# Scores of a cross-attention block: one float32 product per part, or three float32r products of split operands

## The chip, the cores and the metric

The kernel runs on one core of one Trainium2 chip. The metric is the device time of one execution in microseconds (us). Three executions of the kernel before took 1213.2, 1216.02 and 1218.1 us; the median is 1216.02 us.

The engines go by short names: PE is TensorE (PEld its weight loads), DVE is VectorE, ACT is ScalarE, POOL is GpSimd, SP is SyncE, which here does nothing but wait and issue DMAs.

## The reference

`x` has shape (2, 2048, 512), the context (2, 77, 512). One layer is computed:

```python
xn = layernorm(x)
q = (xn @ Wq.T + bq)   # 16 heads of 32
k = (ctx @ Wk.T + bk)
v = (ctx @ Wv.T + bv)
scores = q @ k.T / sqrt(32) + causal      # causal: column s > row t is -inf
x = x + softmax(scores) @ v @ Wo.T + bo
h = silu(q4(layernorm(x)) @ q4(w_gate).T) * (q4(layernorm(x)) @ q4(w_up).T)
out = x + q4(h) @ q4(w_down).T            # q4: blockwise FP4 quantise and dequantise, blocks of 16
```

FF width is 1408. Only the first 77 rows of a batch are touched by the causal mask.

## The kernel before, in words

The 4096 rows are 32 tiles of 128 rows (`T = 32`, 16 per batch). The program has two parts: attention over all 32 tiles (to about 437 us), then the feed-forward part over the same tiles. The change touches the first alone.

Every engine runs its own program, written out by hand; `iteration(a, n)` of an engine is what it does in turn `a`. In one turn several tiles are under way: q is projected for tile `a`, the probabilities of tile `a - 1` are transposed and multiplied by v, the output of tile `a - 2` is projected. Beside that the turn treats weight piece `n = a + 2` of the feed-forward part. There are 33 pieces (`PIECES`), 22 of the gate and up weights (`GU_PIECES`, numbers 0 to 21) and 11 of the down weight (22 to 32). A piece is loaded to `w_in` (two buffers), quantised, transposed by PE, and split into a high and a low half (`piece_high` on ACT, `piece_low` on DVE). Pieces 22 to 32 are split into `wd_out` and stored to HBM by `store_piece`.

What an engine does in a turn, in its own order:

- PE: project q (12 products of 128x512), transpose att, probs, q and the next xn, project out (12 products), scores, probs times v, transpose the piece.
- DVE: `block_max` of the piece (L119), `att_low` (L886), scale, inverse and negated inverse of the piece (L124, L129, L133), `q_bias` (L893), the rounding of the piece (L150, L154, L897 for xn, L159), the residual (L905), `score_max` (L913, L917), statistics, `normalise_att`, `norm_apply`, and last `piece_low` (L952).
- ACT: copy q (L791), `att_high` (L785), three probability copies (L812), the shift of the piece (L145), `xn_high` (L819), 16 exponentials (L829), `piece_high` (L804).
- POOL: divide the piece (L139), rescale it (L165), the row scale and the output bias.
- SP: round `t` of its loop (L501 to L513) issues `load_piece(t + 4)`, `store(t)`, a load of x, and for the down pieces `store_piece(t + 3)` at the round's end. SP takes its list in order: a wait in front holds everything behind it.

A product of the form `split_matmuls` (L169) is three float32r products: high by high, high by low, low by high. In the kernel before the q, output and feed-forward products are made so, while scores (L706) and probs times v (L726) are plain float32. The scores of a tile are five parts (`S_PARTS`): three of 308 columns and two of 154, 1232 in all. The transposed q lies in `qt`, the keys in the block-diagonal `kbd`, filled once at the start by eight DVE operations (L1024).

Of the kernel before, what the change touches and what calls it, by code (L numbers as in the profile page):

```python
# [184 lines left out]
class Setup:  # L185
# [3 lines left out]
    def __init__(self, nc):  # L189
        with ExitStack() as sctx:  # L190
            def row(*tiles):
                sctx.enter_context(nc.sbuf_tensor(f"kept_{tiles[0][0]}", [P, KEPT], F32))
                made = [sctx.enter_context(nc.sbuf_tensor(name, shape, F32)) for name, shape in tiles]
                used = sum(int(np.prod(shape[1:])) for _, shape in tiles)
                sctx.enter_context(nc.sbuf_tensor(f"left_{tiles[0][0]}", [P, ROOM - used], F32))
                return made

            self.w_nat = [row((f"w_nat{i}", [P, EC, E]))[0] for i in range(4)]
            self.wkt, self.wvt = row(("wkt", [P, EC, E]))[0], row(("wvt", [P, EC, E]))[0]
            self.cin, self.ctxT = row(("cin", [CTX, B, E]), ("ctxT", [P, EC, B, CTX]))  # L200
            self.bv_all, self.bias_nat = row(("bv_all", [CTX, E]), ("bias_nat", [EC, 2, P]))

# [127 lines left out]
def attention(nc, keep, k, f, x, ctx_in, Wq, bq, Wk, bk, Wv, bv, Wo, bo, w_gate, w_up, w_down, x1_dram, wd_dram):  # L330

    with ExitStack() as ctx:
# [8 lines left out]
        mask = sb("mask", [P, CTX], BF16)  # L341
        vext = sb("vext", [CTX, B, 2, HALF_HEADS, VW])
        wqh, wql = sb("wqh", [P, EC, E], F32R), sb("wql", [P, EC, E], F32R)
        bqc = sb("bqc", [P, EC])
        bkc = sb("bkc", [P, EC])
        bo_all = sb("bo_all", [P, E])
        kbd = sb("kbd", [P, B, EC, 4 * CTX])
        vbd = sb("vbd", [P, B, 2, PV_CHUNKS, PV_HEADS * VW])
# [11 lines left out]
        w_nat, wkt, wvt, cin, ctxT = k.setup.w_nat, k.setup.wkt, k.setup.wvt, k.setup.cin, k.setup.ctxT  # L360
        bv_all, bias_nat = k.setup.bv_all, k.setup.bias_nat
        with ExitStack() as sctx:
# [5 lines left out]
        q = sb("q", [P, E])  # L368
        qt = sb("qt", [P, EC, P])
        smax = sb("smax", [P, HEADS])  # L370
# [7 lines left out]
        ath, atl = sb("ath", [P, EC, P], F32R), sb("atl", [P, EC, P], F32R)  # L378
        wd_out = sb("wd_out", [P, 2, 2, E], F32R)
        q_ps = ps("q_ps", [P, 512])  # L380
# [8 lines left out]
        small_done, small_ready = sem("small_done"), sem("small_ready")  # L389
        k_done, kbd_ready = sem("k_done"), sem("kbd_ready")  # L390
        v_done, v_ready = sem("v_done"), sem("v_ready")
# [7 lines left out]
        xnT_done, xnh_ready, xnl_ready = sem("xnT_done"), sem("xnh_ready"), sem("xnl_ready")  # L399
        q_done, q_copied, qT_done, q_ready = sem("q_done"), sem("q_copied"), sem("qT_done"), sem("q_ready")  # L400
        s_done, smax_ready, nsmax_ready, probs_ready = (sem(n) for n in ("s_done", "smax_ready", "nsmax_ready", "probs_ready"))
# [31 lines left out]
        def sp_part(sp):  # L433
# [26 lines left out]
            def store_piece(n):  # L460
                c = n - GU_PIECES
                sp.wait_ge(wl_ready, n + 1)
                sp.wait_ge(wh_ready, n + 1)
                if c >= 1:
                    sp.wait_ge(wd_stored, 16 * c)
                sp.dma_start(wd_dram[:, :, c, :], wd_out[:, c % 2].bitcast(F32)).then_inc(wd_stored, 16)

# [23 lines left out]
            sp.wait_ge(const_ready, 3)  # L491
            sp.wait_ge(zeroed, 2)
            for b in range(B):
# [7 lines left out]
            for t in range(T):  # L501

                if t + 4 < PIECES:
                    load_piece(t + 4)
                store(t)

                if t + RING < T:
                    load(t + RING)
                else:
                    f.load(sp, t + RING - T, x1_t[t + RING - T])  # L510

                if GU_PIECES <= t + 3 < PIECES:
                    store_piece(t + 3)  # L513

        def pool_part(pool):
# [40 lines left out]
            pool.memset(vext[:, :, :, :, HD:VW], 1.0).then_inc(const_ready, 1)  # L556
            pool.memset(kbd[:], 0.0).then_inc(zeroed, 1)
            pool.memset(vbd[:], 0.0).then_inc(zeroed, 1)
# [19 lines left out]
        def pe_part(pe, first_gate, first_up):  # L578
# [47 lines left out]
            def project_q(a):  # L626
                pe.wait_ge(xnh_ready, a + 1)
                pe.wait_ge(xnl_ready, a + 1)
                if reached(a):
                    pe.wait_ge(q_ready, a)  # L630
                else:

                    pe.wait_ge(wth_ready, 2 * EC)
                    pe.wait_ge(wtl_ready, EC)
                split_matmuls(pe, q_ps[:], [(xnh[:, d, :], xnl[:, d, :], wqh[:, d, :], wql[:, d, :])
                                            for d in range(EC)]).then_inc(q_done, 1)
# [55 lines left out]
            def scores(a):  # L692
                pe.wait_ge(q_ready, a + 1)
                if reached(a):
                    pe.wait_ge(pT_ready, S_BANKS * a)
                if not reached(a):
                    pe.wait_ge(kbd_ready, 1)
                b = a // TB
                causal = isinstance(a, int) and a % TB == 0
                for i, (c, h0, h1) in enumerate(S_PARTS):  # L700
                    bank, o = h0 // S_HEADS, (h0 % S_HEADS) * CTX
                    out = s_ps[:, bank, o:o + (h1 - h0) * CTX]
                    if causal:
                        pe.matmul(out, ident16[:], mask[:].unsqueeze(1).to_broadcast([P, h1 - h0, CTX]),
                                  start=True, stop=False)
                    last = pe.matmul(out, qt[:, c, :], kbd[:, b, c, (h0 % 4) * CTX:(h0 % 4 + h1 - h0) * CTX],  # L706
                                     start=not causal, stop=True)
                    if i in (1, 3, 4):
                        last.then_inc(s_done, 1)
# [70 lines left out]
        def act_part(act):  # L780
# [6 lines left out]
            def q_copy(t):  # L787
# [3 lines left out]
                act.activation(q[:], q_ps[:], ACT.Copy).then_inc(q_copied, 1)  # L791

            def piece_high(n, down):
                act.wait_ge(wT_done, n + 1)
                if down:
                    c = n - GU_PIECES
                    if isinstance(c, int) and c >= 2:
                        act.wait_ge(wd_stored, 16 * (c - 1))
                    if not isinstance(c, int):
                        act.wait_ge(wd_stored, 16 * (c - 1))  # L800
                    dst = wd_out[:, c % 2, 0, :].rearrange("p (c k) -> p c k", k=P)
                else:
# [30 lines left out]
            def iteration(a, n, down=None):  # L833
# [10 lines left out]
                if valid(a - 1):  # L844
                    probs_copy(a - 1)
                if piece(n):
                    wquant.shift(act, n + 1)
# [12 lines left out]
            def weight_high(i):  # L860
                for n in range(i * EC, (i + 1) * EC):
                    act.wait_ge(wt_done, n + 1)
                    act.activation((wkt, wqh, wvt, woh)[i][:, n % EC, :], tp[:, n % TP, :], ACT.Copy).then_inc(wth_ready, 1)

            weight_high(0)
            weight_high(1)
            xn_high(0)
            wquant.shift(act, 1)
            q_copy(0)
            weight_high(2)  # L870
            piece_high(0, False)
            wquant.shift(act, 2)
# [8 lines left out]
        def dve_part(dve):  # L881
# [6 lines left out]

            def q_bias(t):
                dve.wait_ge(qT_done, t + 1)  # L890
                if reached(t):
                    dve.wait_ge(s_done, S_BANKS * t)
                dve.tensor_tensor(qt[:], q_ps[:].rearrange("p (c k) -> p c k", k=P), bcast(bqc[:], P), ALU.add).then_inc(q_ready, 1)  # L893

# [50 lines left out]
            def piece_low(n, down):  # L945
                dve.wait_ge(wh_ready, n + 1)
                if down:
                    c = n - GU_PIECES
                    high, low = (wd_out[:, c % 2, i, :].rearrange("p (c k) -> p c k", k=P) for i in range(2))
                else:  # L950
# [4 lines left out]
            def iteration(a, n, down=None):  # L955
# [18 lines left out]
                if valid(a):  # L974
                    q_bias(a)
                if piece(n):
# [39 lines left out]
            def keys():  # L1016

                dve.wait_ge(k_done, 1)
                dve.wait_ge(zeroed, 1)
                dve.wait_ge(small_ready, 3)  # L1020
                for b in range(B):
                    for i in range(4):
                        r = slice(i * HD, (i + 1) * HD)
                        last = dve.tensor_tensor(  # L1024
                            kbd[r, b, :, i * CTX:(i + 1) * CTX],
                            kp[r].rearrange("p a (c s) -> p (a c) s", c=2)[:, :, b * CTX:(b + 1) * CTX],
                            bcast(bkc[r, :], CTX), ALU.add)
                last.then_inc(kbd_ready, 1)

# [41 lines left out]
            piece_rounded(0)  # L1071
            q_bias(0)
            piece_scales(1)
# [14 lines left out]

        over = Over(q_done, q_ready, pT_ready, att_ready, wo_done, x1_ready, xb_ready)
        return Parts(sp_part, pool_part, pe_part, act_part, dve_part), over  # L1090


# [485 lines left out]
```

## Time and profile before

| | |
|---|---|
| executions | 1213.2, 1216.02, 1218.1 us |
| profiled execution | 1214.13 us, its span 1212.3 us |
| granted TensorE clock, mean | 0.999 |
| PE busy | 1183.8 us, 98% |
| DVE busy | 970.7 us, 80% |
| ACT busy | 468.3 us, 39% |
| POOL busy | 176.1 us, 15% |
| chain that ended last | PE 91%, DVE 5%, ACT 2% |

Busy is the time in which an engine had an instruction under way. A PE instruction's duration holds its way through the array, and the next begins before it ends, so what a product costs PE in a stream is the distance between two starts. The same holds in smaller measure for DVE and ACT. A plain float32 product is shown as two instructions, a float32r product as one. The chain is followed back from the last instruction of the program to what released each.

### The profile page before, as it was taken

The numbers are of one execution on the slowest core, as the hardware profiler recorded it, in microseconds if no ns is written. First come the engines' busy times: TensorE is split into PE (matmuls) and PEld (weight loads), VectorE is DVE, ScalarE is ACT, GpSimd is POOL, SyncE is SP. The second block draws the span as 40 slices with busy tenths as digits, with TensorE's granted clock in tenths as the row PEclk, the third lists the DMA queues.
The fourth block names the chain that finished last, engine by engine and source line by source line (L and its number), as shares of the span: only waits on it lengthen the run. The fifth ranks groups of instructions, "written<-read, shape, count | busy, mean of one in ns | idle before, by whom it ended". The sixth has DMA issues, their size and how long they took to land.

```text
span 1212.3 us, 21262 instructions
## 1 busy us (share of the span) xinstructions
PE 1183.8 (98%) x6994; PEld 1080.1 (89%) x6994; DVE 970.7 (80%) x1705; ACT 468.3 (39%) x1141; POOL 176.1 (15%) x305
## 2 busy tenths in 40 slices
PE   7899999999999988899999999999999999999998
PEld 6688888888888878799999999999999999999997
DVE  6878888888888865887888788788878878878875
ACT  3556556566565542332232223223223322322321
POOL 3333333333333300000000000000000000000000
PEclk9999999999999999999999999999999999999999
DMA  6112111121232317235224423423432442353240
GB/s 233 29 53 78 52 64 66 52 79 53 93 124 87 115 60 245 39 64 98 57 54 94 69 54 77 87 54 55 103 61 54 91 72 54 67 97 55 54 92 27
DMA packets 91943, 94.33 MB, mean 78 GB/s; under 512 B 54513, under 2 KB 63905, under 8 KB 91784
## 3 DMA queue, kind: packets, MB, share of 16 engines
q1 hardware_dynamic: 91912, 93.95, 32.2%
q8 instruction: 15, 0.25, 0.1%
q14 instruction: 16, 0.13, 0.0%
HBM read 58.48 MB, written 23.94 MB: 68 GB/s over the span
## 4 chain that ended last, share of the span: by engine, by line
PE 91%; DVE 5%; ACT 2%; issue 1%; DMA 1%; SPq 0%; POOL 0%; DVEq 0%; ACTq 0%; POOLq 0%
PE u_ps L174 7%; PE u_ps L175 6%; PE u_ps L176 6%; PE g_ps L174 6%; PE g_ps L175 6%; PE g_ps L176 6%; PE d_ps L1291 6%; PE d_ps L1292 6%; PE d_ps L1293 6%; PE o_ps L726 5%; PE s_ps L706 5%; PE s_ps L671 3%; PE w_ps L174 2%; PE w_ps L175 2%; PE w_ps L176 2%; PE q_ps L176 2%
## 5 line engine op out<-in xcount | busy, mean ns | idle before, releaser
L174 PE MATMUL g_ps<-wguh,xnh 128*128 128x352 f32 x512 | 168.0, 328 | 8.1 <-ACT silu L1332 3.7
L174 PE MATMUL u_ps<-wguh,xnh 128*128 128x352 f32 x512 | 167.6, 327 | 2.1 <-DVE hid L1401 2.1
L1401 DVE TENSOR_TENSOR hid<-u_ps,silu 128x352 f32<-128x352 f32 x128 | 66.7, 521 | 125.1 <-PE u_ps L176 125.1
L175 PE MATMUL u_ps<-wgul,xnh 128*128 128x352 f32 x512 | 165.1, 322 | 0.0
L175 PE MATMUL g_ps<-wgul,xnh 128*128 128x352 f32 x512 | 165.0, 322 | 0.0
L176 PE MATMUL g_ps<-wguh,xnl 128*128 128x352 f32 x512 | 164.6, 322 | 0.0
L176 PE MATMUL u_ps<-wguh,xnl 128*128 128x352 f32 x512 | 164.6, 321 | 0.0
L829 ACT ACTIVATE probs<-s_ps,nsmax 128x77 f32<-128x77 f32 x512 | 114.1, 374 | 99.2 <-DVE nsmax L917 99.2
L1332 ACT ACTIVATE silu<-g_ps 128x352 f32<-128x352 f32 x128 | 58.8, 460 | 215.6 <-PE g_ps L176 210.0
L1291 PE MATMUL d_ps<-wd,hqh 128*128 128x512 f32 x330 | 128.9, 391 | 0.0
L1292 PE MATMUL d_ps<-wd,hqh 128*128 128x512 f32 x330 | 128.8, 390 | 0.0
L1293 PE MATMUL d_ps<-wd,hql 128*128 128x512 f32 x330 | 128.5, 389 | 0.0
L174 PEld LDWEIGHTS g_ps<-wguh,xnh 128*128 128x128 f32 x512 | 96.1, 188 | 11.8 <-ACT silu L1332 4.3
L271 POOL TENSOR_TENSOR nmean<-f_mv,minus_one 128x1 f32<-128x1 f32 x32 | 6.1, 191 | 679.2 <-DVE f_mv L266 679.2
L174 PEld LDWEIGHTS u_ps<-wguh,xnh 128*128 128x128 f32 x512 | 96.1, 188 | 2.7 <-DVE hid L1401 2.7
L175 PEld LDWEIGHTS g_ps<-wgul,xnh 128*128 128x128 f32 x512 | 96.3, 188 | 1.1
L176 PEld LDWEIGHTS u_ps<-wguh,xnl 128*128 128x128 f32 x512 | 96.6, 189 | 0.0
L176 PEld LDWEIGHTS g_ps<-wguh,xnl 128*128 128x128 f32 x512 | 96.4, 188 | 0.0
L175 PEld LDWEIGHTS u_ps<-wgul,xnh 128*128 128x128 f32 x512 | 96.2, 188 | 0.0
L145 ACT ACTIVATE quant_magic<-quant_z 128x512 bf16<-128x512 f32 x65 | 41.0, 631 | 143.0 <-DVE quant_z L139 90.2
L726 PEld LDWEIGHTS o_ps<-vbd,probsT 128*128 128x128 f32 (+1 forms) x640 | 76.5, 191 | 4.4
L726 PE MATMUL o_ps<-vbd,probsT 128*128 128x66 f32 (+2 forms) x640 | 75.0, 272 | 0.0
(146 smaller groups left out, 2539.1 us busy)
## 6 DMA issues: line engine op xcount, KB each, us to landing
scale_wide<-st_dram SPq DMA_DIRECT2D x248, 88.0 KB, 3.9
xin<-in_x_dram SPq DMA_DIRECT2D x32, 256.0 KB, 2.8
x_dram<-x SPq DMA_DIRECT2D x32, 256.0 KB, 2.0
xin<-x_dram SPq DMA_DIRECT2D x32, 256.0 KB, 2.9
out_dram<-y SPq DMA_DIRECT2D x32, 256.0 KB, 2.1
wd_dram<-wd_out SPq DMA_DIRECT2D x11, 512.0 KB, 3.9
wd<-wd_dram SPq DMA_DIRECT2D x1, 5632.0 KB, 17.0
w_in<-in_L_ffn_w_gate_dram SPq DMA_DIRECT2D x11, 256.0 KB, 2.9
```

Source lines behind the costliest of these rows:

```text
L145: s.activation(self.magic[:, part.cols], self.z[:, part.cols], ACT.Copy, scale=ULP_SHIFT).then_inc(self.shifted_ready, 1)
L174: pe.matmul(out, lh, rh, start=(i == 0), stop=False)
L175: pe.matmul(out, lh, rl, start=False, stop=False)
L176: last = pe.matmul(out, ll, rh, start=False, stop=(i == n - 1))
L706: last = pe.matmul(out, qt[:, c, :], kbd[:, b, c, (h0 % 4) * CTX:(h0 % 4 + h1 - h0) * CTX], start=not causal, stop=True)
L726: last = pe.matmul(o_ps[:, half, h0 * VW:(h1 + 1) * VW], probsT[0:rows, i, :], vbd[0:rows, b, half, c, 0:(h1 - h0 + 1) * VW], start=(c == ...
L829: last = act.activation(probs[:, h * CTX:(h + 1) * CTX], s_ps[:, bank, o:o + CTX], ACT.Exp, bias=nsmax[:, h:h + 1], scale=SCALE)
L1291: pe.matmul(total, high[:, c, :], wd[:, 0, c, :], start=(c == 0), stop=False)
L1292: pe.matmul(total, high[:, c, :], wd[:, 1, c, :], start=False, stop=False)
L1293: summed = pe.matmul(total, low[:, c, :], wd[:, 0, c, :], start=False, stop=(c == FC - 1))
L1332: act.activation(silu[:, c % 2, :], g_ps[:, c % 2, 0:GU_N], ACT.Silu).then_inc(silu_ready, 1)
L1401: dve.tensor_tensor(hid[:, c * GU_N:(c + 1) * GU_N], u_ps[:, c % 2, 0:GU_N], silu[:, c % 2, :], ALU.mult).then_inc(hid_ready, 1)
```

## The change

- `scores` makes three float32r products per part, of `qh` and `ql` with `kbh` and `kbl`, in place of one float32 product of `qt` and `kbd`.
- `qt` and `q_bias` go. ACT makes `qh` from the transposed q with the bias added, by four activations of 128x128 (`q_high`, after the probability copies); DVE makes `ql` by four operations of 128x128 (`q_low`, in `q_bias`'s place), after `qh`.
- The keys are first written with their bias to `kf` (one DVE operation), then copied to `kbh` by eight ACT copies, then `kbl` is made by eight DVE operations. One more memset runs on POOL.
- `wd_out` has one buffer and not two. `piece_high` of a down piece waits until the piece before is stored, and SP's `store_piece(t + 3)` stands at the head of round `t`, ahead of `load_piece(t + 4)`.

```diff
-        qt = sb("qt", [P, EC, P])
+        qh, ql = sb("qh", [P, EC, P], F32R), sb("ql", [P, EC, P], F32R)
-        wd_out = sb("wd_out", [P, 2, 2, E], F32R)
+        wd_out = sb("wd_out", [P, 2, E], F32R)
...
             for t in range(T):
 
+                if GU_PIECES <= t + 3 < PIECES:
+                    store_piece(t + 3)
                 if t + 4 < PIECES:
                     load_piece(t + 4)
                 store(t)
...
-                if GU_PIECES <= t + 3 < PIECES:
-                    store_piece(t + 3)
...
-            pool.memset(kbd[:], 0.0).then_inc(zeroed, 1)
+            pool.memset(kbh[:].bitcast(F32), 0.0).then_inc(zeroed, 1)
+            pool.memset(kbl[:].bitcast(F32), 0.0).then_inc(zeroed, 1)
...
             def scores(a):
-                pe.wait_ge(q_ready, a + 1)
+                pe.wait_ge(qh_ready, a + 1)
+                pe.wait_ge(ql_ready, a + 1)
...
-                    last = pe.matmul(out, qt[:, c, :], kbd[:, b, c, (h0 % 4) * CTX:(h0 % 4 + h1 - h0) * CTX],
-                                     start=not causal, stop=True)
+                    cols = slice((h0 % 4) * CTX, (h0 % 4 + h1 - h0) * CTX)
+                    pe.matmul(out, qh[:, c, :], kbh[:, b, c, cols], start=not causal, stop=False)
+                    pe.matmul(out, qh[:, c, :], kbl[:, b, c, cols], start=False, stop=False)
+                    last = pe.matmul(out, ql[:, c, :], kbh[:, b, c, cols], start=False, stop=True)
...
+            def q_high(t):
+                act.wait_ge(qT_done, t + 1)
+                if reached(t):
+                    act.wait_ge(s_done, S_BANKS * t)
+                for c in range(EC):
+                    last = act.activation(qh[:, c, :], q_ps[:, c * P:(c + 1) * P], ACT.Identity, bias=bqc[:, c:c + 1], scale=1.0)
+                last.then_inc(qh_ready, 1)
...
-                    if isinstance(c, int) and c >= 2:
-                        act.wait_ge(wd_stored, 16 * (c - 1))
-                    if not isinstance(c, int):
-                        act.wait_ge(wd_stored, 16 * (c - 1))
-                    dst = wd_out[:, c % 2, 0, :].rearrange("p (c k) -> p c k", k=P)
+                    if reached(c):
+                        act.wait_ge(wd_stored, 16 * c)
+                    dst = wd_out[:, 0, :].rearrange("p (c k) -> p c k", k=P)
...
+            def keys():
+
+                act.wait_ge(kf_ready, 1)
+                act.wait_ge(zeroed, 2)
+                for b in range(B):
+                    for i in range(4):
+                        r = slice(i * HD, (i + 1) * HD)
+                        last = act.activation(kbh[r, b, :, i * CTX:(i + 1) * CTX], kf[r, :, b * CTX:(b + 1) * CTX], ACT.Copy)
+                last.then_inc(kbh_ready, 1)
...
             weight_high(0)
             weight_high(1)
             xn_high(0)
             wquant.shift(act, 1)
+            keys()
             q_copy(0)
             weight_high(2)
+            q_high(0)
...
-            def q_bias(t):
-                dve.wait_ge(qT_done, t + 1)
+            def q_low(t):
+                dve.wait_ge(qh_ready, t + 1)
                 if reached(t):
                     dve.wait_ge(s_done, S_BANKS * t)
-                dve.tensor_tensor(qt[:], q_ps[:].rearrange("p (c k) -> p c k", k=P), bcast(bqc[:], P), ALU.add).then_inc(q_ready, 1)
+                for c in range(EC):
+                    last = dve.scalar_tensor_tensor(out=ql[:, c, :], in0=q_ps[:, c * P:(c + 1) * P], scalar=bqc[:, c:c + 1],
+                                                    in1=qh[:, c, :].bitcast(F32), op0=ALU.add, op1=ALU.subtract)
+                last.then_inc(ql_ready, 1)
...
+                dve.tensor_tensor(kf[:], kp[:].rearrange("p a (c s) -> p (a c) s", c=2)[:, :, 0:B * CTX],
+                                  bcast(bkc[:], B * CTX), ALU.add).then_inc(kf_ready, 1)
+
+            def keys_low():
+
+                dve.wait_ge(kbh_ready, 1)
                 for b in range(B):
                     for i in range(4):
                         r = slice(i * HD, (i + 1) * HD)
...
+                        cols = slice(i * CTX, (i + 1) * CTX)
+                        last = dve.tensor_tensor(kbl[r, b, :, cols], kf[r, :, b * CTX:(b + 1) * CTX],
+                                                 kbh[r, b, :, cols].bitcast(F32), ALU.subtract)
+                last.then_inc(kbl_ready, 1)
...
             keys()
             norm_apply(1)
             piece_rounded(0)
-            q_bias(0)
+            keys_low()
+            q_low(0)
```

## Rows read from the trace of the kernel before

**Rows 1.** Busy time, nine turns from 299.46 to 413.91 us: sum and mean of each engine.

```profile
sum 114.45, PE 114.45 PEld 100.86 DVE 94.73 ACT 68.33 POOL 37.11; mean PE 12.72 PEld 11.21 DVE 10.53 ACT 7.59 POOL 4.12
```

**Rows 2.** Timeline of SP: start us, duration us, line, what is issued.

```profile
294.77 0.41 SPq L458 DMA_DIRECT2D w_in<-in_L_ffn_w_down_dram  x1
...
332.99 0.53 SPq L466 DMA_DIRECT2D wd_dram<-wd_out  x1
333.60 0.56 SPq L458 DMA_DIRECT2D w_in<-in_L_ffn_w_down_dram  x1
```

**Rows 3.** Timeline of DVE, one turn and the next's head; in brackets the idle before.

```profile
299.38 0.68 DVE L119 TENSOR_REDUCE quant_amax<-w_in 128x32 f32<-128x512 f32 x1
300.43 0.69 DVE L886 TENSOR_TENSOR atl<-w_ps,ath 128x512 fp32r<-128x512 f32 x1 [0.38 <-ACT ath L785]
...
301.63 0.18 DVE L133 TENSOR_SCALAR quant_ninv<-quant_inv 128x32 f32<-128x32 f32 x1
301.73 0.68 DVE L893 TENSOR_TENSOR qt<-q_ps,bqc 128x512 f32<-128x512 f32 x1
303.65 0.29 DVE L150 TENSOR_SCALAR quant_magic<-quant_magic 128x512 int16<-128x512 int16 x1 [1.24 <-ACT quant_magic L145]
...
311.41 0.69 DVE L952 TENSOR_TENSOR wd_out<-xn_ps,wd_out 128x512 fp32r<-128x512 f32 x1 [0.36 <-ACT wd_out L804]
312.42 0.69 DVE L119 TENSOR_REDUCE quant_amax<-w_in 128x32 f32 x1 [0.32 <-DMA w_in<-in_L_ffn_w_down_dram]
```

**Rows 4.** DMA issues, 240 to 360 us: count, KB each, median us to landing.

```profile
wd_dram<-wd_out SPq DMA_DIRECT2D x5, 512.0 KB, 3.9
w_in<-in_L_ffn_w_down_dram SPq DMA_DIRECT2D x7, 256.0 KB, 4.1
```

**Rows 5.** The same view, 230 to 290 us, where no store goes ahead.

```profile
w_in<-in_L_ffn_w_down_dram SPq DMA_DIRECT2D x1, 256.0 KB, 3.1
```

**Rows 6.** The chain that ended last, piece by piece: start us, us, what, instructions.

```profile
15.85 4.20 PE kp L614 x32
...
299.71 1.09 PE s_ps L671 x10
...
304.43 2.08 PE s_ps L706 x10
```

**Rows 7.** Timeline of PE, float32r products of 352 columns in a stream.

```profile
701.29 0.32 PE L174 MATMUL g_ps<-wguh,xnh 128*128 128x352 f32 x1
701.45 0.32 PE L175 MATMUL g_ps<-wgul,xnh 128*128 128x352 f32 x1
```

**Rows 8.** Timeline of ACT and PE around the transposed q of one turn.

```profile
294.69 3.56 ACT L829 ACTIVATE probs<-s_ps,nsmax 128x77 f32<-128x77 f32 x16 [3.21 <-DVE nsmax L917]
...
300.29 1.37 ACT L812 ACTIVATE probsT<-s_ps 128x512 f32<-128x512 f32 x3
...
300.64 0.60 PE L641 MATMUL q_ps<-ident,q 128*128 128x128 f32 x4
...
302.99 0.63 ACT L145 ACTIVATE quant_magic<-quant_z 128x512 bf16<-128x512 f32 x1 [1.33 <-POOL quant_z L139]
```

**Rows 9.** Timeline of the start: POOL, DVE and ACT.

```profile
1.91 2.15 POOL L557 MEMSET kbd<- 128x2464 f32 x1
...
9.05 0.19 POOL L520 TENSOR_TENSOR veps<-mv,eps 128x1 f32<-128x1 f32 x1 [3.31 <-DVE mv L936]
...
20.09 3.90 DVE L1024 TENSOR_TENSOR kbd<-kp,bkc 32x308 f32<-32x308 f32 x8 [0.45 <-PE kp L614]
...
22.88 0.60 ACT L791 ACTIVATE q<-q_ps 128x512 f32<-128x512 f32 x1 [1.43 <-PE q_ps L176]
```

**Rows 10.** Timeline of PE at the first long idle time.

```profile
11.93 0.47 PE L594 MATMUL tp<-ident,w_nat 128*128 128x128 f32 x1 [2.97 <-DMA w_nat<-in_L_xattn_Wq_dram]
```

**Rows 11.** Windows: stretch, busy PE, PEld, DVE, ACT, POOL, then granted clock.

```profile
12.00:16.00 4.00, 4.00 (x23) 3.83 (x24) 1.97 (x3) 2.35 (x5) 0.00 (x0) 0.62 1.05 372
494.00:498.00 4.00, 0.72 (x5) 0.43 (x4) 3.86 (x8) 2.54 (x5) 0.00 (x0) 1.00 0.00 0
```

More of the change, by code:

```diff
@@ L199, in __init__ @@
             self.wkt, self.wvt = row(("wkt", [P, EC, E]))[0], row(("wvt", [P, EC, E]))[0]
-            self.cin, self.ctxT = row(("cin", [CTX, B, E]), ("ctxT", [P, EC, B, CTX]))
-            self.bv_all, self.bias_nat = row(("bv_all", [CTX, E]), ("bias_nat", [EC, 2, P]))
+            self.cin, self.ctxT, self.kf = row(("cin", [CTX, B, E]), ("ctxT", [P, EC, B, CTX]), ("kf", [P, EC, B * CTX]))
+            self.bv_all, self.bias_nat, self.vext = row(
+                ("bv_all", [CTX, E]), ("bias_nat", [EC, 2, P]), ("vext", [CTX, B, 2, HALF_HEADS, VW]))
 class Shared:
@@ L341, in attention @@
         mask = sb("mask", [P, CTX], BF16)
-        vext = sb("vext", [CTX, B, 2, HALF_HEADS, VW])
         wqh, wql = sb("wqh", [P, EC, E], F32R), sb("wql", [P, EC, E], F32R)
@@ L346, in attention @@
         bo_all = sb("bo_all", [P, E])
-        kbd = sb("kbd", [P, B, EC, 4 * CTX])
+        kbh, kbl = sb("kbh", [P, B, EC, 4 * CTX], F32R), sb("kbl", [P, B, EC, 4 * CTX], F32R)
         vbd = sb("vbd", [P, B, 2, PV_CHUNKS, PV_HEADS * VW])
@@ L360, in attention @@
         w_nat, wkt, wvt, cin, ctxT = k.setup.w_nat, k.setup.wkt, k.setup.wvt, k.setup.cin, k.setup.ctxT
-        bv_all, bias_nat = k.setup.bv_all, k.setup.bias_nat
+        bv_all, bias_nat, vext, kf = k.setup.bv_all, k.setup.bias_nat, k.setup.vext, k.setup.kf
         with ExitStack() as sctx:
@@ L389, in attention @@
         small_done, small_ready = sem("small_done"), sem("small_ready")
-        k_done, kbd_ready = sem("k_done"), sem("kbd_ready")
+        k_done, kf_ready, kbh_ready, kbl_ready = sem("k_done"), sem("kf_ready"), sem("kbh_ready"), sem("kbl_ready")
         v_done, v_ready = sem("v_done"), sem("v_ready")
@@ L399, in attention @@
         xnT_done, xnh_ready, xnl_ready = sem("xnT_done"), sem("xnh_ready"), sem("xnl_ready")
-        q_done, q_copied, qT_done, q_ready = sem("q_done"), sem("q_copied"), sem("qT_done"), sem("q_ready")
+        q_done, q_copied, qT_done, qh_ready, ql_ready = (sem(n) for n in (
+            "q_done", "q_copied", "qT_done", "qh_ready", "ql_ready"))
         s_done, smax_ready, nsmax_ready, probs_ready = (sem(n) for n in ("s_done", "smax_ready", "nsmax_ready", "probs_ready"))
@@ L465, in store_piece @@
                     sp.wait_ge(wd_stored, 16 * c)
-                sp.dma_start(wd_dram[:, :, c, :], wd_out[:, c % 2].bitcast(F32)).then_inc(wd_stored, 16)
+                sp.dma_start(wd_dram[:, :, c, :], wd_out[:].bitcast(F32)).then_inc(wd_stored, 16)
             def load_weight(i, w):
@@ L491, in sp_part @@
             sp.wait_ge(const_ready, 3)
-            sp.wait_ge(zeroed, 2)
+            sp.wait_ge(zeroed, 3)
             for b in range(B):
@@ L629, in project_q @@
                 if reached(a):
-                    pe.wait_ge(q_ready, a)
+                    pe.wait_ge(qh_ready, a)
+                    pe.wait_ge(ql_ready, a)
                 else:
@@ L696, in scores @@
                 if not reached(a):
-                    pe.wait_ge(kbd_ready, 1)
+                    pe.wait_ge(kbh_ready, 1)
+                    pe.wait_ge(kbl_ready, 1)
                 b = a // TB
@@ L845, in iteration @@
                     probs_copy(a - 1)
+                if valid(a):
+                    q_high(a)
                 if piece(n):
@@ L948, in piece_low @@
                     c = n - GU_PIECES
-                    high, low = (wd_out[:, c % 2, i, :].rearrange("p (c k) -> p c k", k=P) for i in range(2))
+                    high, low = (wd_out[:, i, :].rearrange("p (c k) -> p c k", k=P) for i in range(2))
                 else:
@@ L974, in iteration @@
                 if valid(a):
-                    q_bias(a)
+                    q_low(a)
                 if piece(n):
@@ L1018, in keys @@
                 dve.wait_ge(k_done, 1)
-                dve.wait_ge(zeroed, 1)
                 dve.wait_ge(small_ready, 3)
+                dve.tensor_tensor(kf[:], kp[:].rearrange("p a (c s) -> p (a c) s", c=2)[:, :, 0:B * CTX],
+                                  bcast(bkc[:], B * CTX), ALU.add).then_inc(kf_ready, 1)
+            def keys_low():
+                dve.wait_ge(kbh_ready, 1)
                 for b in range(B):
@@ L1023, in keys @@
                         r = slice(i * HD, (i + 1) * HD)
[L1024 to L1028, printed above, removed]
+                        cols = slice(i * CTX, (i + 1) * CTX)
+                        last = dve.tensor_tensor(kbl[r, b, :, cols], kf[r, :, b * CTX:(b + 1) * CTX],
+                                                 kbh[r, b, :, cols].bitcast(F32), ALU.subtract)
+                last.then_inc(kbl_ready, 1)
             def values(b):
@@ L1087, in dve_part @@
             run(dve, iteration, 1)
-        over = Over(q_done, q_ready, pT_ready, att_ready, wo_done, x1_ready, xb_ready)
+        over = Over(q_done, ql_ready, pT_ready, att_ready, wo_done, x1_ready, xb_ready)
         return Parts(sp_part, pool_part, pe_part, act_part, dve_part), over
```

## The prediction

> **What bounds the kernel now.** I read the page's shares first. PE is busy 98% of the span and 91% of the chain that ended last, so a change pays by what it does to PE, or by making PE wait. The change lies in the attention part alone, so I then read the windows of nine of its turns. There PE is busy 114.45 of 114.45 us, 12.72 per turn, while DVE is busy 10.53, ACT 7.59 and POOL 4.12 [rows 1]. PE never waits, but DVE is not far off. Third, the timeline of DVE. From the piece's `block_max` at 299.38 to the end of `piece_low` at 311.41 + 0.69 = 312.10 pass 12.72 us, and the next `block_max` follows at once. Inside lie three waits: 0.38 for ACT's `ath`, 1.24 for the shifted piece (the way DVE, POOL, ACT, DVE), and 0.36 for ACT's `piece_high` [rows 3]. The last two belong to DVE's own loop through POOL and ACT; only the first is for PE's pace. So PE's loop of 12.72 and DVE's of about 12.3 run side by side with 0.4 us between them. Whatever adds more than that to DVE's loop bounds the kernel in place of PE.
>
> **SP's order, the largest term.** In the kernel before, the load of the down piece that DVE maximises at 299.38 is issued at 294.77, 4.6 us ahead [rows 2, 3]. After the change round `t` begins with `store_piece(t + 3)`, which waits for `wl_ready`, the end of `piece_low` of piece t + 3; that is the last thing that DVE does in its turn. Behind it in SP's list stands `load_piece(t + 4)`, and `block_max` of that very piece is the next thing that DVE does. So nothing of the load is hidden any more. This holds for t = 19 to 28, which load pieces 23 to 32: ten loads. The price of one:
>
> - from the end of `piece_low`, SP starts the store, and the load is issued 333.60 - 332.99 = 0.61 us later [rows 2];
> - the load lands 4.1 us after its issue where a 512 KB store and two more transfers go ahead of it, and 3.1 us where no store does [rows 4, 5]. Here only the store goes ahead. I take 3.5, between the two, and keep both ends;
> - about 0.1 us for the two hand-overs.
>
> Together 4.2 us (3.8 to 4.8) from the end of `piece_low` to the next `block_max`. From there DVE's loop takes 12.72 less the 0.38 for `ath`, which will be long ready: 12.34. A turn is then 16.55 us against 12.72, 3.8 more. Behind the waiting `block_max` stand `att_low`, then all of DVE's turn; PE waits for `atl` before it projects out, as `att_low` ends at 301.12 and PE's project out begins only 0.3 us later. Ten turns give 38 us, less that 0.3 once. The earlier loads of a gate or up piece are not touched, since SP stores nothing for them. That DVE already waits 0.32 us for such a load in one turn shows how little room is left even now [rows 3]. The single `wd_out` buffer costs ACT nothing: the store lands some 4 us after `piece_low`, and ACT's next write to it comes after 16 exponentials, over 10 us later [rows 4, 8].
>
> **The scores on PE.** Before, a tile's scores take 2.08 us on PE [rows 6]: 1232 columns in four passes, 0.42 ns per column and pass. After, there are 15 products of one pass each. A float32r product of 352 columns costs 0.160 us between two starts [rows 7]; 147 of these 160 ns are its columns at 0.417 ns, 13 are fixed. One of 308 columns then costs 0.142, nine 1.28. A product of 154 columns would cost 0.078 by that, but each needs a weight load of 128 columns, and where PE does nothing but short products with such loads, ten take 1.09 us, 0.109 each [rows 6]. I take 0.109: six cost 0.65. The sum is 1.93, so a tile saves 0.15 us. The ends: 0.078 (1.75 in all, 0.33 saved) and, since no float32r product shorter than 352 columns is in the trace, 0.160 for every one (2.40, 0.32 lost). It counts only where PE sets the pace: 32 tiles, less the ten above, less the first two, in which DVE and ACT set it, so 20 tiles: 3 us saved (6.6 saved to 6.4 lost).
>
> Plain float32 takes four passes here and three are put in place, so one may count passes alone. The Trainium skill, "FP8 and Floating Point Precision", section "TensorE Precision Notes", says this of float32: four passes through the array, of high and low halves. The trace agrees, with 0.42 ns per column and pass. Three passes for four would make 1.56 of 2.08 us; that is rival B.
>
> **The halves of q.** `q_high` follows the three probability copies on ACT, which end at 300.29 + 1.37 = 301.66; the transposes of q end at 301.24 [rows 8]. An activation of 77 columns costs 0.22 (3.56 / 16), one of up to 512 columns 0.46 (1.37 / 3). I take 0.25 for 128 columns: four end at 302.7. ACT is idle there, 1.33 us until its shift at 302.99 [rows 8], so nothing on ACT is delayed. A DVE operation of 32 columns lasts 0.18, `q_bias` with 512 lasts 0.68 [rows 3]; on a line between them 128 columns last 0.28, four 1.1, to 303.8. DVE idles from 302.41 to 303.65 for the shifted piece anyway [rows 3], so its loop grows by 0.15 at most, within its 0.4. PE wants `ql` at 304.43 [rows 6], 0.6 us later. I cost this at nothing. At 0.46 and 0.35 per operation `ql` would be ready at 304.9 and PE would lose 0.5 in each of 20 tiles, 10 us: the upper end.
>
> **The start.** DVE's eight operations on the keys take 3.90 us [rows 9]; they remain as `keys_low`, and one of 616 columns, some 0.8 us, comes ahead. Between them ACT makes eight copies of 308 columns, at 0.22 to 0.46 each, I take 0.35: 2.8 us, from 20.9 to 23.7 or a little later. The copy of q, which begins at 22.88 [rows 9], and the v weights behind it come about 1 us later, and DVE's `q_low(0)` and all behind it wait for `keys_low`. The start is one chain over all engines, so I add 1.5 us (0 to 4.4, where all is serial). POOL's second memset adds 2.15, but POOL then idles 3.31 us before its next work [rows 9]: nothing.
>
> **Sum.** 38 - 3 + 1.5 = 36.5 on the profiled execution of 1214.1 us (span 1212.3), so 1250.6. The median of the runs stands 1.9 above that execution, hence **1252.5 us**. Own range, with the landing at either end (-4, +6), the start (-1.5, +3) and the scores (-4, +9): 1243 to 1265.
>
> **Rivals.**
>
> A. The short float32r parts don't run at one pass. Nothing in the trace shows such a product under 352 columns. If one of 154 columns takes as long as the plain one (two instructions of 0.131 each, 4.20 / 32 [rows 6]), six take 1.57, the scores 2.85 and a tile loses 0.77, 15 us over 20 tiles in place of 3 saved: 1271.
>
> B. Three quarters of the passes in three quarters of the time: 0.52 saved in each of 20 tiles, 10 us: 1245. Against it stand the 0.109 us per load.
>
> C. The clock. In each of the ten turns PE has 12.6 us of work in 16.55, so it idles some 3.9 us in one piece before it projects out. After 2.97 us of idle time at the start the granted clock fell to half, 0.62 on the mean of the next 4 us [rows 10, 11]. But from 494 to 498 us PE was busy 0.72 of 4.00 and the clock stayed at 1.00 [rows 11]. A fall costs (1 - 0.62) x 4 = 1.5 us of PE's work, which the 3.9 us of idle time cover; if none of it were covered, ten falls add 15: 1268.
> The Trainium skill, "TensorE: Matmul & The Clock Gate", section "HAM oscillation — how this bites in real kernels", says that a kernel which waits before each burst of products starts every burst at the low clock. By that all ten turns fall; of the two idle times here one agrees and one does not.
>
> D. Not slower. The load is hidden after all: SP would have to pass its wait for `piece_low` over 4.2 us before `block_max`. Everything up to 3.8 us of delay per turn then vanishes, and 1216 - 3 + 1.5 = 1214.5 remains. Even if the short products cost 0.078 that makes 1211, barely 0.5% faster. For it speaks that DVE has 1.24 us of idle time in its turn; against it that this lies in a loop of its own.
>
> **Chances.** Forecast 0.59, A 0.22, B 0.07, C 0.06, D 0.05, others 0.01. A range of 1240 to 1276 takes in the forecast, A to its middle and beyond, B and C. Slower by over 0.5% (6 us, about what can be told from no change): 0.94; within: 0.03; faster: 0.03.
>
> **What would show it.** In the changed profile DVE's `block_max` waits 4 us for the DMA of the down piece, ten times, and PE's project out waits for `atl` as often. Turns of about 16.5 us in the down pieces and of 12.6 before them. L706's successors take 1.9 us a tile, 2.85 under A, 1.56 under B; `ql` is ready before PE wants it. If turns with down pieces keep 12.7 us, SP's order was read wrongly; if all turns grow alike, the halves of q or A are the cause.

## The result, and the profile after

The changed kernel took 1267.1 to 1269.89 us in four runs, median 1268.99, against 1215.14 us for the kernel before in the same runs: a ratio of 1.0439 (95% interval 1.0413 to 1.0465), 53.9 us slower. The forecast was 1252.5 us with a range of 1240 to 1276.

| | before | after |
|---|---|---|
| median | 1215.14 us | 1268.99 us |
| profiled execution, its span | 1214.13, 1212.3 us | 1268.25, 1266.5 us |
| mean granted clock | 0.999 | 0.977 |
| PE busy | 1183.8 us, 98% | 1205.2 us, 95% |
| chain: PE, DVE, DMA | 91%, 5%, 1% | 79%, 7%, 4% |

I took the end of every `piece_low` in both traces as milestones. They place the 54.1 us of span:

| stretch | before | after | difference |
|---|---|---|---|
| start to piece 3 | 59.05 | 63.09 | +4.0 |
| the turn of piece 4 | 12.17 | 14.83 | +2.7 |
| pieces 4 to 22 | 228.25 | 226.27 | -2.0 |
| pieces 22 to 32, ten turns | 127.03 | 174.34 | +47.3 |
| the rest | 785.8 | 787.9 | +2.1 |

**The ten turns.** The timeline of SP and DVE after, at one of them:

```profile
338.55 0.69 DVE L982 TENSOR_TENSOR wd_out<-xn_ps,wd_out 128x512 fp32r<-128x512 f32 x1
...
339.27 0.53 SPq L467 DMA_DIRECT2D wd_dram<-wd_out  x1
...
339.89 0.56 SPq L459 DMA_DIRECT2D w_in<-in_L_ffn_w_down_dram  x1
...
343.79 0.69 DVE L119 TENSOR_REDUCE quant_amax<-w_in 128x32 f32 x1 [4.54 <-DMA w_in<-in_L_ffn_w_down_dram]
344.39 0.68 DVE L913 TENSOR_TENSOR atl<-w_ps,ath 128x512 fp32r<-128x512 f32 x1
```

`piece_low` (L982) ends at 339.24, SP stores at 339.27, loads at 339.89, and DVE's next operation waits 4.54 us for that load. In [rows 2, 3] the load went out 4.6 us ahead. The waits of all ten turns, and the DMA issues with the time to landing:

```profile
DVE quant_amax L119 <- DMA w_in<-in_L_ffn_w_down_dram: 45.8, 10, 5.0
...
PE w_ps L174 <- DVE atl L913: 30.3, 10, 3.9
```

```profile
wd_dram<-wd_out SPq DMA_DIRECT2D x10, 512.0 KB, 3.4
w_in<-in_L_ffn_w_down_dram SPq DMA_DIRECT2D x10, 256.0 KB, 3.7
```

The chain of waits leaves PE and goes through the load (start, us, what):

```profile
338.55 0.70 DVE wd_out L982
339.27 0.53 SPq L467
...
339.89 3.69 DMA w_in<-in_L_ffn_w_down_dram
...
344.39 0.68 DVE atl L913
...
346.01 1.07 POOL quant_z L139
347.11 0.64 ACT quant_magic L145
347.77 0.31 DVE quant_magic L150
```

**The scores.** PE's timeline in a turn in which it sets the pace:

```profile
207.92 0.30 PE L712 MATMUL s_ps<-kbh,qh 128*128 128x308 f32 x1
208.06 0.30 PE L713 MATMUL s_ps<-kbl,qh 128*128 128x308 f32 x1
208.20 0.31 PE L714 MATMUL s_ps<-kbh,ql 128*128 128x308 f32 x1
208.35 0.23 PE L712 MATMUL s_ps<-kbh,qh 128*128 128x154 f32 x1
208.42 0.27 PE L713 MATMUL s_ps<-kbl,qh 128*128 128x154 f32 x1
208.53 0.28 PE L714 MATMUL s_ps<-kbh,ql 128*128 128x154 f32 x1
208.64 0.28 PE L712 MATMUL s_ps<-kbh,qh 128*128 128x154 f32 x1
208.75 0.28 PE L713 MATMUL s_ps<-kbl,qh 128*128 128x154 f32 x1
...
209.87 0.92 PE L733 MATMUL o_ps<-vbd,probsT 128*128 128x66 f32 x7
```

Read the starts, not the durations: a short product costs 0.11 us, one of 308 columns 0.14. The scores take 1.95 us, from 207.92 to 209.87, against 2.08 in [rows 6], and a turn in a stream of such turns 12.53 against 12.64.

**The halves of q**, in a turn like that, from the timelines of ACT and DVE:

```profile
205.19 1.17 ACT L805 ACTIVATE qh<-q_ps,bqc 128x128 fp32r<-128x128 f32 x4
```

```profile
205.40 0.18 DVE L133 TENSOR_SCALAR quant_ninv<-quant_inv 128x32 f32<-128x32 f32 x1
206.50 1.13 DVE L921 SCALAR_TENSOR_TENSOR ql<-q_ps,bqc,qh 128x128 fp32r<-128x128 f32 x4 [0.91 <-ACT qh L805]
207.59 0.30 DVE L150 TENSOR_SCALAR quant_magic<-quant_magic 128x512 int16<-128x512 int16 x1
```

DVE's idle time of 1.24 us ahead of L150 [rows 3] is gone: 0.91 us of it is now the wait for `qh`, the rest is `q_low`. L150 begins 2.0 us after the end of L133, against 1.84 before. It costs the steady turn nothing, but nothing is left there.

**The start.** ACT's key copies, and what stands behind them; then PE in turn 1:

```profile
21.17 3.77 ACT L887 ACTIVATE kbh<-kf 32x308 fp32r<-32x308 f32 x8
24.96 0.60 ACT L798 ACTIVATE q<-q_ps 128x512 f32<-128x512 f32 x1
```

```profile
54.17 0.38 PE L712 MATMUL s_ps<-kbh,qh 128*128 128x308 f32 x1 [2.40 <-DVE ql L921]
```

The copy of q begins 2.1 us later than in [rows 9]. In turn 1, where nothing on PE hides the way from the transposed q over ACT and DVE, PE waits 2.40 us for `ql`. In the kernel before it waited 1.15 for `qt`:

```profile
49.55 2.35 PE L706 MATMUL s_ps<-kbd,qt 128*128 128x308 f32 x10 [1.15 <-DVE qt L893]
```

Behind the wait of 2.40 us the granted clock fell. The windows (stretch, busy PE, PEld, DVE, ACT, POOL, then the clock):

```profile
52.00:56.00 4.00, 1.82 (x14) 1.86 (x15) 3.23 (x10) 2.03 (x6) 1.06 (x1) 0.98 0.30 79
56.00:60.00 4.00, 4.00 (x20) 4.00 (x20) 3.76 (x11) 2.35 (x12) 1.22 (x2) 0.50 0.00 1
60.00:64.00 4.00, 4.00 (x18) 3.54 (x18) 2.68 (x6) 1.81 (x7) 1.87 (x3) 0.67 0.00 0
```

From 56 to 60 us PE ran at 1.2 GHz. That lies in the turn of piece 3; PE's lost work reaches DVE in the next one, which took 14.83 us at a granted clock of 1.00.

The filler experiment below separates the longer chain of the start from the clock. Its kernel is the changed one until turn 21, and PE has the same wait, but in its trace the clock stayed:

```profile
54.03 0.38 PE L712 MATMUL s_ps<-kbh,qh 128*128 128x308 f32 x1 [2.40 <-DVE ql L925]
```

```profile
56.00:60.00 4.00, 4.00 (x32) 3.77 (x31) 3.76 (x11) 2.49 (x12) 1.27 (x3) 1.00 0.10 34
```

There piece 3 ends at 62.29 and piece 4 at 74.54, where the changed trace has 63.09 and 77.92 and the kernel before 59.05 and 71.22. So of the 6.7 us lost up to piece 4, 3.3 are there without a fall and 3.4 come with two, this one and one at 42 us. These are single traces: the first `piece_low` alone ends between 32.4 and 33.4 us in the five traces whose start is that of the changed kernel.

### The profile page after: what moved, and what is told of

Same layout as the page of the kernel before. It is cut to its first block, busy times and chain, and to the rows that moved or that the text cites. A ratio compares the mean times of both kernels' runs of the same rounds, so it can differ in the third digit from the quotient of the medians.

```text
span 1266.5 us, 21834 instructions
## 1 busy us (share of the span) xinstructions
PE 1205.2 (95%) x7154; PEld 1107.8 (87%) x7154; DVE 987.6 (78%) x1802; ACT 505.4 (40%) x1277; POOL 178.3 (14%) x306
## 4 chain that ended last, share of the span: by engine, by line
PE 79%; DVE 7%; ACT 4%; DMA 4%; issue 3%; POOL 1%; SPq 1%; DVEq 0%; POOLq 0%; ACTq 0%
PE g_ps L174 6%; PE u_ps L174 6%; PE u_ps L175 6%; PE u_ps L176 6%; PE g_ps L175 6%; PE g_ps L176 6%; PE d_ps L1326 6%; PE d_ps L1327 6%; PE d_ps L1328 6%; PE o_ps L733 4%; DMA w_in<-in_L_ffn_w_down_dram 3%; ACT probs L842 3%; PE w_ps L174 2%; PE w_ps L176 2%; PE w_ps L175 2%
## 5 line engine op out<-in xcount | busy, mean ns | idle before, releaser
L174 PE MATMUL w_ps<-woh,ath 128*128 128x512 f32 x128 | 60.1, 469 | 30.3 <-DVE atl L913 30.3
```

What stands on the lines that cost most here:

```text
L174: pe.matmul(out, lh, rh, start=(i == 0), stop=False)
```

## Experiments

Each ran beside the kernel before on the same chip. The first four kernels ran on one chip, where before's median was 1216.21 us, the last four on another, where it was 1215.33. Across the two, ratios to the kernel before are compared.

### SP's order alone

The kernel before with this and nothing else of the change (`piece_high` and `piece_low` address the one buffer):

```diff
-        wd_out = sb("wd_out", [P, 2, 2, E], F32R)
+        wd_out = sb("wd_out", [P, 2, E], F32R)
             for t in range(T):
+                if GU_PIECES <= t + 3 < PIECES:
+                    store_piece(t + 3)
                 if t + 4 < PIECES:
                     load_piece(t + 4)
```

> The kernel before with one part of the change alone: a single wd_out buffer and store_piece(t + 3) at the head of SP's round. Theory (SP's order makes ten loads of down pieces fully exposed): the ten turns grow from 12.7 to about 17.2 us, the start stays as before, so 1215 + 10 x 4.5 = 1260 (1256 to 1264). Rival (the halves of q and the float32r scores cost the time in those turns): within 5 us of the kernel before.

Measured: 1262.75 us, ratio 1.0388 (1.0363 to 1.0414), 46.5 us slower. Its ten turns take 173.03 us against 174.34 in the changed kernel, its start is as before (piece 3 at 59.01).

```profile
DVE quant_amax L119 <- DMA w_in<-in_L_ffn_w_down_dram: 45.7, 10, 5.0
```

The same wait, without any half of q or float32r score. So SP's order makes 46.5 of the 53.9 us by itself, the falls of the clock that it brings included: the mean granted clock of these ten turns is 0.89.

### The load first

The changed kernel with two lines exchanged:

```diff
-                if GU_PIECES <= t + 3 < PIECES:
-                    store_piece(t + 3)
                 if t + 4 < PIECES:
                     load_piece(t + 4)
+                if GU_PIECES <= t + 3 < PIECES:
+                    store_piece(t + 3)
```

> The changed kernel with the two lines of SP's round exchanged: load_piece(t + 4), then store_piece(t + 3). Theory: no exposed load, every turn from the fourth on 12.5 us; what stays against the kernel before is the start (+6.5 us in the changed trace) less 0.11 us in each of some 28 turns: 1215 + 6.5 - 3 = 1218 (1215 to 1221). Rival (halves or short products weigh on the down turns as well): 1235 or more, with down turns over 13.5 us.

Measured: 1219.24 us, ratio 1.0030 (1.0017 to 1.0043). The ten turns take 125.37 us, 1.7 less than before the change, and DVE waits for no load:

```profile
299.58 0.69 DVE L982 TENSOR_TENSOR wd_out<-xn_ps,wd_out 128x512 fp32r<-128x512 f32 x1 [0.35 <-ACT wd_out L817]
300.19 0.68 DVE L119 TENSOR_REDUCE quant_amax<-w_in 128x32 f32<-128x512 f32 x1
```

With the order undone 49.7 us come back. The single buffer costs nothing.

### The price of an exposed load, split

```diff
+                if GU_PIECES <= t + 3 < PIECES:
+                    sp.wait_ge(wl_ready, t + 4)
                 if t + 4 < PIECES:
                     load_piece(t + 4)
                 if GU_PIECES <= t + 3 < PIECES:
                     store_piece(t + 3)
```

> The changed kernel, but SP waits for piece_low, then issues the load, then the store. Splits the price of an exposed load. Theory (the store ahead costs its issue of 0.6 us and delays the landing from 3.1 to 3.7): DVE's wait falls from 4.5 to 3.3 us, 10 x 1.2 = 12 less, 1257. Rival (the landing does not depend on the store ahead): 0.6 less each, 1263.

Measured: 1250.69 us, ratio 1.0285 (1.0262 to 1.0309), 18.3 less than the changed kernel. The load without the store ahead, and the wait:

```profile
w_in<-in_L_ffn_w_down_dram SPq DMA_DIRECT2D x10, 256.0 KB, 2.9
```

```profile
DVE quant_amax L119 <- DMA w_in<-in_L_ffn_w_down_dram: 31.3, 10, 3.3
```

The wait fell from 4.58 us on the mean (45.8 / 10) to 3.13 (31.3 / 10), 1.45 each: 0.6 for the store's issue and 0.8 of landing. That is more than either theory had, and the ten turns fell by 18.7 us, not 14.5. The other 4.2 us fit the clock, which fell in five of these turns and not in ten: less the wait a turn takes 12.44 us here and 12.85 in the changed kernel. Over half of it, 2.2 us, lies in the first and the last of the ten.

### The falls of the clock

Twelve products whose result nobody reads, on PE ahead of its project out:

```diff
+                if down or (isinstance(a, int) and 21 <= a <= 31):
+                    for i in range(12):
+                        pe.matmul(o_ps[:, 0, :], wqh[:, i % EC, 0:P], wqh[:, i % EC, :], start=True, stop=True,
+                                  skip_group_check=True)
                 if valid(a - 2):
                     project_out(a - 2)
```

> The changed kernel with 12 more products of 128x512, thrown away, on PE before it projects out in turns 21 to 31: 2.7 us of work in idle time of 2.9 us. Prices the falls of the clock. Theory (the falls delay the projection and the scores, on which DVE's residual and score maximum wait): the granted clock stays at 1.00 in these turns, DVE's loop from block_max to piece_low goes from 12.7 to 12.35, 4 us less in all: 1265. Rival (the idle time covers the falls): clock 1.00, time unchanged, 1269.

Measured: 1262.41 us, ratio 1.0387 (1.0363 to 1.0412), 6.6 less than the changed kernel, with 12 products more per turn. The ten turns of the changed kernel, then of this one, with the clock after the POOL column:

```profile
304.19:478.53 174.34, 144.06 (x845) 126.62 (x844) 109.93 (x281) 85.88 (x281) 40.86 (x52) 0.88 0.24 75
```

```profile
300.82:470.30 169.48, 155.16 (x973) 136.16 (x972) 108.87 (x281) 86.04 (x282) 40.81 (x52) 1.00 0.25 78
```

The wait for the load is unchanged (46.0 us in all). The turns without that wait take (169.48 - 46.0) / 10 = 12.35 us, and with the falls (174.34 - 45.8) / 10 = 12.85. So ten falls cost 5 us, near the theory's 4, and the rival is out. DVE's timelines show where: ahead of the residual (`x`), which reads PE's projection, DVE idles in the changed kernel and not with the filler (the profile names no releaser for it):

```profile
367.53 0.69 DVE L935 TENSOR_TENSOR x<-w_ps,xin 128x512 f32 x1 [0.25 <-issue]
```

```profile
362.29 0.68 DVE L939 TENSOR_TENSOR x<-w_ps,xin 128x512 f32 x1
```

The price isn't the same in each turn. In the eight middle turns, whose granted clock is 0.90, a fall costs 0.3 us; in the first and the last, with 0.81 and 0.82, it costs 1.1 and 1.5 and makes half of the sum. The other 1.7 us of the difference lie outside the ten turns: in this profile the clock didn't fall in the start either, and the turn of piece 4 took 12.25.

### The later keys

On top of the load first, ACT's `keys(1)` (batch 1) moves to turn 1 and DVE's four operations on it to turns 2 and 3:

```diff
+                if isinstance(a, int) and a == 1:
+                    keys(1)
...
+                if isinstance(a, int) and a in (2, 3):
+                    keys_low(1, range(2 * a - 4, 2 * a - 2))
```

> Load-first kernel, and the halves of batch 1's keys are made later: ACT's four copies in turn 1, where it waits for the score maxima, DVE's four operations in turns 2 and 3. Theory (the start's loss is the chain of key copies on ACT and DVE, ahead of q's copy and the v weights): 1.9 us of copies leave the chain, piece_low of piece 3 ends some 2 us earlier than with load first alone (61.8 us), 1217 against 1219. Rival (the loss lies elsewhere, in the larger kf step or the halves of q): no earlier, 1219.

Measured: 1216.33 us, ratio 1.0008 (0.9999 to 1.0018). Piece 3 ends at 60.79, 1.0 us earlier than with the load first alone, not 2. Even that isn't shown to be the keys' doing. In the load-first trace the clock fell once on the way, and the turn of piece 2 took 8.22 us against 7.76 here. And the two traces with the load first and all keys made at once (the other is that of the next experiment) place the end of piece 3 at 61.77 and 62.43. The next three turns cost as much again (38.8 us against 37.7), since DVE has no idle time left behind `q_low`:

```profile
64.64 0.94 DVE L1065 TENSOR_TENSOR kbl<-kf,kbh 32x308 fp32r<-32x308 f32 x2
```

The ratio is 0.2% lower all the same, on another chip. The two profiles don't show why: their spans are 1214.0 and 1213.6 us, but the first profile is that kernel's fastest run. What the runs differ in is told below; this one is not settled.

### A filler in turn 1

```diff
+                if isinstance(a, int) and a == 1:
+                    for i in range(8):
+                        pe.matmul(o_ps[:, 0, :], wqh[:, i % EC, 0:P], wqh[:, i % EC, :], start=True, stop=True,
+                                  skip_group_check=True)
                 if valid(a):
                     scores(a)
```

> Load-first kernel with 8 products of 128x512, thrown away, on PE ahead of the scores of turn 1, where PE waits 2.4 us for ql. Theory (part of the loss against the kernel before is the granted clock, which falls after that wait in some executions): mean clock of the runs rises from 0.992 to about 0.995, median 1217.5 and a narrower spread. Rival (the clock at the start costs nothing): 1219.

Measured, on the load-first kernel: 1216.11 us, ratio 1.0006 (0.9997 to 1.0015), the runs' mean clock 0.994. 0.24% less than load first alone, whose runs had a mean clock of 0.992. Unrounded the two clocks lie 0.0027 apart, which makes, as an estimate, 3 us of 1216, as much as the times differ. So the clock can account for all of it. That the eight products raised it isn't shown. The load-first kernel without them ran on the other chip only, and on this one the later-keys kernel, which has no filler, had the same mean clock and the same time (0.994, 1216.33 us). In the load-first trace the clock stayed behind the wait in turn 1 anyway, and in the trace with the filler it fell elsewhere, at 43, 439 and 500 us.

### The short parts plain

On top of the later keys, the parts of 154 columns are one plain float32 product, with q and keys of that head group unsplit (`q1`, `kb1`), so DVE makes three `ql` operations in place of four:

```diff
+                    if c == 1:
+                        last = pe.matmul(out, q1[:], kb1[:, b, cols], start=not causal, stop=True)
+                    else:
+                        pe.matmul(out, qh[:, c, :], kbh[:, b, pos[c], cols], start=not causal, stop=False)
+                        pe.matmul(out, qh[:, c, :], kbl[:, b, pos[c], cols], start=False, stop=False)
+                        last = pe.matmul(out, ql[:, c, :], kbh[:, b, pos[c], cols], start=False, stop=True)
```

> The kernel with the later keys, and the two parts of 154 columns (head group 1) as one plain float32 product each, with q and keys of that group unsplit; the three parts of 308 columns stay in three float32r products. Theory (a short float32r product is bound by its weight load at 0.111 us, so three cost 0.333 and one plain one 0.260): the scores fall from 1.95 to 1.80 us, turns from 12.53 to 12.38, 28 x 0.15 = 4 less: 1213. Rival (DVE's loop of about 12.3 to 12.4 us takes over): turns of 12.45 or more, 1215.

Measured: 1213.10 us, ratio 0.9978 (0.9968 to 0.9987). The scores from PE's timeline:

```profile
152.89 0.30 PE L725 MATMUL s_ps<-kbh,qh 128*128 128x308 f32 x1
...
153.31 0.69 PE L723 MATMUL s_ps<-kb,q 128*128 128x154 f32 x4
153.73 0.41 PE L725 MATMUL s_ps<-kbh,qh 128*128 128x308 f32 x1
...
154.69 0.58 PE L746 MATMUL o_ps<-vbd,probsT 128*128 128x66 f32 x4
```

From 152.89 to 154.69 are 1.80 us, as expected. The down turns take 12.39 against 12.54; the gate and up turns only 12.49 against 12.53, though PE is busy throughout in both. The scores gain 0.15 in those too, but the transposes of xn, the last work before PE's projection out, take 0.44 in place of 0.36. That points to DVE, as the rival had it: in these turns the projection begins 0.15 us after `atl` ends, as in the ten turns of the changed kernel in which PE waits for it, and in the down turns 0.19. The rest, 0.03, is spread over PE's products and stays open. And both additions together:

> The two together: short parts plain, later keys, and the 8 thrown-away products in turn 1. Theory: 1 to 2 less than the short-plain kernel, 1212, below the kernel before. Rival (the later keys have already removed the wait that the products fill): equal to the short-plain kernel or 0.5 slower.

Measured: 1211.63 us, ratio 0.9969 (0.9957 to 0.9981), 0.3% faster than the kernel before and 4.5% faster than the changed one. It has the lowest median of all versions; the intervals of its ratio and of the short-plain kernel's overlap, and its mean clock was 0.996 against 0.994.

## Why the prediction was right, and where it was off

The mechanism was right, and it made most of the loss. That the time lies within 1240 to 1276 is in part luck: the range reached so far up for rival A, which is out, and the forecast's own range ended at 1265. By the time alone, 1268.99 is nearer to rival A's 1271 and rival C's 1268 than to the forecast of 1252.5; it is the profile and the experiments that tell them apart.

**SP's order, forecast 38 us.** Right in its mechanism, in the number of turns and in the place; the ten turns grew by 47.3 us. Three terms, by their measured sizes:

- the wait for the load, forecast 4.2 us, was 4.58 on the mean (45.8 / 10). The landing was 3.7 and not the 3.5 between the two bounds, and the hand-over before DVE's operation is 0.2 us, not a part of 0.1. That is 4 us.
- DVE's loop, forecast 12.34, is 12.35 when the clock stands (the filler experiment): exact.
- the clock's falls, forecast at nothing in the main case and given to rival C, took place in all ten turns and cost 5 us in all. So rival C, at a chance of 0.06, had the event right, and its upper end of 15 three times too high; the main case had the event wrong. The step that failed is "which the 3.9 us of idle time cover". The idle time does cover the lost work of PE as a sum, but not in order: PE projects out right after its wait, at half clock, and DVE's residual stands behind the projection. DVE idles some 0.25 us ahead of it in a middle turn, 0.8 and 0.9 in the first and the last.

**The scores, forecast 3 us saved.** 1.93 forecast for the scores, 1.95 measured; 0.109 for a short product, 0.11 measured. A turn gained 0.11, not 0.15: 2 us over pieces 4 to 22. Rivals A (the short products at four passes) and B (three quarters of the time) are out. B's rule, counting passes as the Trainium skill's "FP8 and Floating Point Precision", section "TensorE Precision Notes", lets one do, leaves out the weight load that comes with each product.

**The halves of q, forecast at nothing.** Right for the steady turn: `q_high` 1.17 us (forecast 1.0), `q_low` 1.13 (1.1), and PE never waits for `ql` there. Wrong for turn 1, to which I carried the cover of a steady turn: there PE waits 2.40 us.

**The start, forecast 1.5 us, upper end 4.4.** This step failed most in proportion: 4.0 up to piece 3 and 2.7 more in the next turn. About half of it, 3.3, is the longer chain, within the bounds: the key copies cost 0.47 us each, at the upper end and not 0.35, 3.77 in place of 2.8. The other half, 3.4, came with falls of the clock, which were not among the terms of the start at all.

**Rival D** is out: the exposed load is in all ten turns, and gone with the order alone.

The forecast was 16.5 us under the median: some 9 in the ten turns, 5 in the start and the turn behind it, 1 in the scores, 2 in the rest, less 1 for the median of before, which came out at 1215.14 and not 1216.02. The 2 in the rest are mostly not of the change. They lie in the end of the attention part, where PE waits 2.0 us for `att` in place of 1.5, and in a fall of the clock at 551 us. The trace with SP's order alone has that fall too, the wait of 1.5 as before, and a rest of 787.8 us; the traces of all nine other kernels have a fall at that place of the program, the one trace of the kernel before has none.

**The range.** The recorded own range of 1243 to 1265 doesn't follow from its ends: 6, 3 and 9 us above 1252.5 make 1270.5. The 10 us that late halves of q could have cost are in neither.

## What to carry to other kernels

When a buffer is halved and a store is moved up to free it, look at what the store waits for and at what stands behind it in the issuing engine's list: here a load whose user is the very next operation after that wait, and the whole memory latency came onto the path, ten times. Issue the load first; it is one exchange of lines. And where a product is short, compare the weight load with the columns: one plain float32 product of 154 columns costs 0.26 us, three float32r products 0.33.

## What was not expected of the hardware

- An idle time of 2.7 to 3.9 us on PE in each turn brought the clock down in each of ten turns, while one of 3.28 at 497.76 us did not in the kernel before. With 1.3 to 1.9 us of idle time (the filler) it never fell in those turns. The length of the idle time alone doesn't decide: at some 40 us, 1.8 us of it brought the clock down in the trace with SP's order alone and not in the kernel before, and the 2.40 us of turn 1 brought it down in the changed trace and not in the filler's. In the kernel that waits, loads and then stores, falls and full-speed turns mostly alternate: after a turn with a fall PE idles only 1.5 us, and the clock stays; then it idles 2.7 again. The Trainium skill, "TensorE: Matmul & The Clock Gate", section "HAM oscillation — how this bites in real kernels", describes a low clock at each burst behind a wait; the changed trace agrees, with a mean clock of 0.88 over the ten turns.
- The time of a run goes with its mean clock. Of 28 runs of the kernel before, the two at 0.993 took 1218.6 and 1218.9 us, the three at 0.999 1213.2 to 1214.2; it isn't the whole of it, since the twelve at 0.997 spread from 1213.9 to 1217.2. For differences under 0.5% the clock of each run has to be read beside its time, and products that compute nothing can make a kernel faster, as the filler did to the changed one (ratio 1.0387 against 1.0439).
